# A graph network's last stage: scaled rows written into PSUM by VectorE, fewer tiles on GpSimd, shorter lags

## The reference, cut to what matters

```
out = node_feat + out                       # [10000, 512]
mean = out.mean(axis=0)
var = jnp.mean(jnp.square(out - mean), axis=0)
out = (out - mean) * jax.lax.rsqrt(var + EPS) * gamma + beta
...
x = _layernorm(x + out, axis=-1)            # the final result
```

## Time and profile before

| what | us |
|---|---|
| three timed runs | 1425.49, 1428.08, 1439.34 |
| their median | 1428.08 |
| span of the profiled execution, first to last instruction | 1427.3 |
| the last stage in it, about | 1267 to 1427 |

### The profile page before, as it was taken

How to read it: one execution, slowest core, us unless ns; L and a number is a source line. 1 busy time by engine, 2 the same in 40 slices (tenths; PEclk the granted TensorE clock), 3 DMA queues, 4 the chain that set the end, 5 groups by cost and what they waited for, 6 DMA issues and landing times. The chain is left out here.

```text
span 1427.3 us, 22061 instructions
## 1 busy us (share of the span) xinstructions
PE 1338.5 (94%) x6660; PEld 1074.8 (75%) x6660; DVE 1094.3 (77%) x2043; ACT 592.2 (41%) x1107; POOL 824.9 (58%) x766
## 2 busy tenths in 40 slices
PE   7889899999999769999999999999999999859897
PEld 6677778877778658888888888888888888634443
DVE  6468547888888713778888888888888888968787
ACT  3467544555555501222222223222222223246786
POOL 3456425666666533456556666666666665458785
PEclk9999999999999979999999999999999999879999
DMA  8689765666666341344444444444444443849855
GB/s 275 219 295 314 244 243 168 219 221 220 220 215 226 140 141 45 107 131 134 133 134 134 133 133 133 133 133 133 133 133 133 133 133 93 284 162 373 299 194 185
DMA packets 128302, 257.97 MB, mean 181 GB/s; under 512 B 21459, under 2 KB 21907, under 8 KB 128114
## 3 DMA queue, kind: packets, MB, share of 16 engines
q1 hardware_dynamic: 97490, 175.31, 36.9%
q0 software_dynamic: 29920, 80.38, 18.1%
q10 hardware_dynamic: 832, 1.57, 0.3%
HBM read 197.18 MB, written 73.60 MB: 190 GB/s over the span
## 5 line engine op out<-in xcount | busy, mean ns | idle before, releaser
L206 PE MATMUL ps<-w_lo,w_hi 128*128 128x512 f32 (+2 forms) x1140 | 416.6, 365 | 22.0 <-DVE w_lo L1470 18.0
L207 PE MATMUL ps<-w_hi,w_lo 128*128 128x512 f32 (+2 forms) x1140 | 410.7, 360 | 0.0
L208 PE MATMUL ps<-w_hi 128*128 128x512 f32 (+2 forms) x1140 | 410.4, 360 | 0.0
L206 PEld LDWEIGHTS ps<-w_lo,w_hi 128*128 128x128 f32 x1140 | 217.5, 191 | 54.9 <-DVE w_lo L1470 18.4
L208 PEld LDWEIGHTS ps<-w_hi 128*128 128x128 f32 x1140 | 217.0, 190 | 32.3
L207 PEld LDWEIGHTS ps<-w_hi,w_lo 128*128 128x128 f32 x1140 | 217.8, 191 | 29.8
L1216 POOL TENSOR_TENSOR acc_x<-acc_x,node_rows 128x512 f32<-128x512 f32 x72 | 117.0, 1625 | 76.1 <-DMA node_rows<-x_table 71.9
L910 POOL TENSOR_TENSOR node_y<-node_z,node_x 128x512 f32<-128x512 f32 x79 | 101.9, 1290 | 100.1 <-issue 79.3
L206 PE MATMUL ps<-w_lo,agg_hi 128*128 128x512 f32 x316 | 125.5, 397 | 0.0
L208 PE MATMUL ps<-w_hi,agg_hi 128*128 128x512 f32 x316 | 125.5, 397 | 0.0
L207 PE MATMUL ps<-w_hi,agg_lo 128*128 128x512 f32 x316 | 125.4, 397 | 0.0
(11 more groups left out here) (264 smaller groups left out, 2928.2 us busy)
## 6 DMA issues: line engine op xcount, KB each, us to landing
node_x<-in_x SPq DMA_DIRECT2D x79, 256.0 KB
x_table<-node_x SPq DMA_DIRECT2D x79, 256.0 KB, 2.1
node_rows<-x_table SPq DMA_DIRECT2D x79, 256.0 KB, 8.1
coef_all<-coef_table SPq DMA_DIRECT2D x38, 512.0 KB
edge_part<-part SPq DMA_DIRECT2D x40, 256.0 KB
out_dram<-rows_over_w_lo SPq DMA_DIRECT2D x40, 256.0 KB
node_x<-in_ea SPq DMA_DIRECT2D x38, 256.0 KB
msg_table<-dst_rows_and_msg SPq DMA_DIRECT2D x38, 256.0 KB
```

What stands on the lines that cost most here:

```text
L206: pe.matmul(to, left[0], right[1], start=first, stop=False)
L207: pe.matmul(to, left[1], right[0], start=False, stop=False)
L208: return pe.matmul(to, left[0], right[0], start=False, stop=last)
```

## The change

For 59 of 79 tiles VectorE now writes u * scale into the PSUM bank, and TensorE accumulates `shift` and x1 on top of it, without u. The other 20 tiles (j % 4 == 2) are scaled in SBUF by GpSimd with a copy of the scale row, which ScalarE makes; for them TensorE sums shift, x1 and u. GpSimd adds nothing any more. Seven matmuls write every bank once at the start of the stage, so that later ones accumulate. The statistics follow after 2 steps in place of 3, the reciprocals after 4 in place of 6, the roots after 8 in place of 10 and the outputs after 11 in place of 12. The two biases of a pair are one instruction.

```diff
-    PAIR, NORM = 10, 12
-    ADD = 4
+    PAIR, NORM = 8, 11
+    STATS, PAIRED = 2, 4
+    LATE = 4
...
         def by_pool(j):
-            return j % 8 in (1, 4, 6)
+            return j % 4 == 2
...
 # GpSimd
-                for k in range(NT + ADD):
+                for k in range(NT + LATE):
                     if k < NT:
                         pool.wait_ge(u_ok, k + 1)
-                        wait(pool, us_ok, k - R + 1)
                         nc.gpsimd.indirect_dma_start(out=u(k), ...)
-                    j = k - ADD
+                    j = k - LATE
                     if j >= 0 and by_pool(j):
-                        pool.wait_ge(us_ok, j + 1)
-                        nc.gpsimd.tensor_tensor(u(j), u(j), x1(j), ALU.add).then_inc(add_ok, 1)
+                        pool.wait_ge(wide_ok, SCALE_ROW)
+                        pool.wait_ge(u_in[j % R], u_before[j % R] + 16 * (j // R + 1))
+                        nc.gpsimd.tensor_tensor(u(j), u(j), scale_row[:], ALU.mult).then_inc(pool_ok, 1)
...
 # TensorE
+                def write_whole(to):
+                    pe.matmul(to[:], g.w(g.w_hi, WO, 0, 0, P), g.w(g.w_hi, WO, 0), start=True, stop=True).then_inc(open_ok, 1)
+
+                for whole in sum_banks[0:5]:
+                    write_whole(whole)
                 pe.wait_ge(sums_ok, 2)
...
+                pe.wait_ge(split_ok, 6)
+                for whole in sum_banks[5:7]:
+                    write_whole(whole)
                 pe.wait_ge(shift_ok, K)
 
                 for j in range(NT):
-                    wait(pe, norm_ok, j - 6)
-                    pe.matmul(bank(j), ones_r[:], shift, start=True, stop=False)
                     if by_pool(j):
-                        pe.wait_ge(add_ok, pool_adds(j))
+                        wait(pe, norm_ok, j - 6)
+                        pe.wait_ge(u_ok, j + 1)
+                        pe.matmul(bank(j), ones_r[:], shift, start=True, stop=False)
+                        pe.matmul(bank(j), g.ident[:], x1(j), start=False, stop=False)
+                        pe.wait_ge(pool_ok, scaled_by_pool(j))
+                        pe.matmul(bank(j), g.ident[:], u(j), start=False, stop=True).then_inc(sum_ok, 1)
                     else:
                         pe.wait_ge(u_ok, j + 1)
-                        pe.matmul(bank(j), g.ident[:], x1(j), start=False, stop=False)
-                        pe.wait_ge(us_ok, j + 1)
-                    pe.matmul(bank(j), g.ident[:], u(j), start=False, stop=True).then_inc(sum_ok, 1)
+                        pe.wait_ge(us_ok, scaled_in_psum(j))
+                        pe.matmul(bank(j), ones_r[:], shift, start=False, stop=False)
+                        pe.matmul(bank(j), g.ident[:], x1(j), start=False, stop=True).then_inc(sum_ok, 1)
...
 # ScalarE
+                act.wait_ge(wide_ok, SCALE_IN_PSUM)
+                nc.scalar.copy(scale_row[:], scale[:]).then_inc(wide_ok, 1)
                 for k in range(AHEAD, NT + NORM):
...
-                        act.wait_ge(scale_ok, 3 * (j // 2) + 2 + j % 2)
+                        act.wait_ge(scale_ok, 2 * (j // 2) + 2)
...
 # VectorE
-                dve.wait_ge(wide_ok, 1)
-                for k in range(NT + 7):
+                dve.wait_ge(wide_ok, SCALE_ROW)
+                dve.wait_ge(open_ok, 7)
+                for k in range(NT + PAIRED + 1):
                     j = k
-                    if j < NT:
+                    if j < NT and not by_pool(j):
                         dve.wait_ge(u_in[j % R], u_before[j % R] + 16 * (j // R + 1))
-                        v.tensor_tensor(u(j), u(j), scale[:], ALU.mult).then_inc(us_ok, 1)
-                    done = k - 6
+                        wait(dve, norm_ok, j - 6)
+                        v.tensor_tensor(bank(j), u(j), scale[:], ALU.mult).then_inc(us_ok, 1)
+                    done = k - PAIRED
...
-                    j = k - 3
+                    j = k - STATS
...
-                        for i in range(m, m + n):
-                            v.tensor_scalar(bias[:, i, :], mv[:, i, 0:1], rstd[:, i, :], -1.0, ALU.mult, ALU.mult).then_inc(scale_ok, 1)
+                        v.scalar_tensor_tensor(bias[:, m:m + n, :], mv[:, m:m + n, 0:1], -1.0, rstd[:, m:m + n, :], ALU.mult, ALU.mult).then_inc(scale_ok, 1)
```

More of the change, by code:

```diff
@@ L1798, in finish_stage @@
         ones_r = sb(ctx, "fin_ones", [P, P], F32R)
+        scale_row = sb(ctx, "fin_scale_row", [P, D])
         stats = sb(ctx, "fin_stats", [P, RM, 6])
@@ L1839, in finish_stage @@
         u_before = [landed(NT - 1 - s, 0, 0, 4) for s in range(4)] + [32 * ET // 4] * 2 + [32 * NB // 2] * 2
-        us_ok, add_ok, sum_ok, stat_ok, root_ok, scale_ok, norm_ok = (sem(n) for n in (
-            "fin_u_scaled", "fin_u_and_x_added", "fin_y_summed", "fin_stat", "fin_root_ok", "fin_scale_ok", "fin_norm"))
+        us_ok, pool_ok, sum_ok, stat_ok, root_ok, scale_ok, norm_ok = (sem(n) for n in (
+            "fin_u_scaled_in_psum", "fin_u_scaled_by_pool", "fin_y_summed", "fin_stat", "fin_root_ok", "fin_scale_ok", "fin_norm"))
+        open_ok = sem("fin_banks_written")
+        SCALE_IN_PSUM, SCALE_ROW = 1, 2
         y_out = g.w_in[2:6] + g.row_out + g.u_out
@@ L1899, in _ @@
                 pe.matmul(ps[2][:, 0:K], mirror[:], lo[:, 1, :], start=True, stop=True).then_inc(mirrored, 1)
+                pe.wait_ge(split_ok, 6)
+                for whole in sum_banks[5:7]:
+                    write_whole(whole)
                 pe.wait_ge(shift_ok, K)
                 for j in range(NT):
-                    wait(pe, norm_ok, j - 6)
-                    pe.matmul(bank(j), ones_r[:], shift[:].rearrange("p k n -> p (k n)"), start=True, stop=False)
                     if by_pool(j):
-                        pe.wait_ge(add_ok, pool_adds(j))
+                        wait(pe, norm_ok, j - 6)
+                        pe.wait_ge(u_ok, j + 1)
+                        pe.matmul(bank(j), ones_r[:], shift[:].rearrange("p k n -> p (k n)"), start=True, stop=False)
+                        pe.matmul(bank(j), g.ident[:], x1(j), start=False, stop=False)
+                        pe.wait_ge(pool_ok, scaled_by_pool(j))
+                        pe.matmul(bank(j), g.ident[:], u(j), start=False, stop=True).then_inc(sum_ok, 1)
                     else:
                         pe.wait_ge(u_ok, j + 1)
-                        pe.matmul(bank(j), g.ident[:], x1(j), start=False, stop=False)
-                        pe.wait_ge(us_ok, j + 1)
-                    pe.matmul(bank(j), g.ident[:], u(j), start=False, stop=True).then_inc(sum_ok, 1)
+                        pe.wait_ge(us_ok, scaled_in_psum(j))
+                        pe.matmul(bank(j), ones_r[:], shift[:].rearrange("p k n -> p (k n)"), start=False, stop=False, skip_group_check=True)
+                        pe.matmul(bank(j), g.ident[:], x1(j), start=False, stop=True, skip_group_check=True).then_inc(sum_ok, 1)
             @block.scalar
@@ L2007, in _ @@
                     if pair:
-                        dve.wait_ge(scale_ok, done // 2 + done // 2 * 2 + 1)
-                        for i in range(m, m + n):
-                            v.tensor_scalar(bias[:, i, :], mv[:, i, 0:1], rstd[:, i, :], -1.0, ALU.mult, ALU.mult).then_inc(scale_ok, 1)
+                        dve.wait_ge(scale_ok, done // 2 * 2 + 1)
+                        v.scalar_tensor_tensor(bias[:, m:m + n, :], mv[:, m:m + n, 0:1], -1.0, rstd[:, m:m + n, :], ALU.mult, ALU.mult).then_inc(scale_ok, 1)
                     if 0 <= j < NT:
```

6 lines of the change are left out of this document (4 added, 2 removed).

## The result

The change did not make the kernel faster. The ratio to the kernel before is 1.0038, with a 95% interval of 1.0020 to 1.0056 (medians 1438.03 and 1431.12 us, 20 runs each): by the ratio some 5 us slower, where 12 faster were forecast.

A forecast was written before the change was run, and what follows sets the result against it. GpSimd's queue was taken to set the pace, 1.746 us a tile. Gather 8 at 1283.1 plus 116.4 gives 1399.5; plus 8.6 and 6.9 makes 1415.0, with 0.8 for the runs' median 1416 us, range 1409 to 1425.

The forecast's parts named there:

- gathers 8 to 78: GpSimd's main term: 70 gathers at 1.31 and 17 operations at 1.16 make 111.4 us, plus 5 lost, 116.4.
- What could be late next: Check of other engines and new waits: TensorE 1.31 and VectorE 1.33 us a tile, both under GpSimd's 1.60.
- The paragraph on the Trainium skill: Two rules: SBUF contention leaves GpSimd's operation at 1.28 us; a TensorE left without work risks losing its full clock.
- Rival C: GpSimd's multiply costs 1.625 us, or the coupled lags cost as much: 6.8 us more, 1423; chance 0.12.
- signs of being wrong: GpSimd waiting for copies late, its waits before 1345 passing 8 us in sum, or TensorE's clock under 1.00 after 1290.
- its new pace: GpSimd in the steady part: (3 x 1.31 + 2.47)/4 = 1.60 us a tile, from 1.746.
- the price of the early bank writes: Stage start: five bank writes on TensorE ahead of the column totals delay VectorE's first step by 0.7 us (0 to 1).
- The start: Stage start to gather 8: at 1283.1 in place of 1284.28, a net gain of 1.2 us (bounds -1 and 2).
- VectorE's need: Steady part: two tiles fall from 3.05 to 2.66 us, 1.33 a tile, with the PSUM multiply taken as 0.66.
- The stalls before 1350: GpSimd's lost time in the first part, with DMA engines full: 5 us, one more than before.
- Rival A: The stalls vanish, since GpSimd no longer waits behind VectorE: 5 us less, 1411; chance 0.20.
- Rival B: Full DMA engines hold the first part at its old length, gather 43 staying at 1350.42: 1422 us; chance 0.19.

The follow-up runs named there:

- e1: The changed kernel with the merged bias undone, again two tensor_scalar instructions; ratio 0.9901 to the kernel before, pace 1.603 us a tile.
- e5: The changed kernel with all tiles scaled by VectorE, none by GpSimd, and two biases in place of the merged one; ratio 0.9881 to the kernel before.
- e6: The changed kernel with two biases again, plus an idle scalar_tensor_tensor with two small SBUF tensors that nobody reads; ratio 1.0048 to the kernel before.
- e14: The changed kernel with two biases, plus an idle scalar_tensor_tensor whose second tensor is read from PSUM; ratio 0.9862 to the kernel before.
- e10: The changed kernel with two biases, GpSimd scaling one tile of six, and the early bank writes behind the column totals; ratio 0.9887 to the kernel before.
- e4: The kernel before with only the shorter lags and its two biases; ratio 0.9987 to the kernel before.
- e12: The changed kernel with two biases and lags near the old ones (statistics 3, reciprocals 5, roots 10, outputs 12 steps); ratio 1.0010 to the kernel before.

## Why the prediction was wrong

The terms of the sum, each from the trace:

| term | forecast | changed | e1 |
|---|---|---|---|
| stage start to gather 8 | 15.8 | 17.2 | 17.2 |
| gathers 8 to 78 | 116.4 | 130.6 | 112.6 |
| gather 78 to the last statistics | 8.6 | 11.2 | 8.7 |
| to the end | 6.9 | 6.2 | 6.2 |
| stage | 147.7 | 165.2 | 144.7 |

**The step that failed** is "What could be late next", where the bias stands only as a gain: "one bias of about 0.1". Both halves of it were wrong. The gain is nothing, since the biases lie between statistics and aggregate (e5). And the merged instruction is the one new instruction with two SBUF tensors on VectorE beside a GpSimd that works on SBUF. Held, it took 1.74 us too long about every fourth tile. Between gathers 8 and 78 the changed kernel is 18.0 us longer than e1 and 14.2 longer than the forecast; in the tail it is 2.5 longer than e1. e1, e6 and e14 show this from three sides: without it the forecast's pace is there (1.603 against 1.60), the idle copy of it alone brings the loss back, and with one operand in PSUM it costs nothing.

The paragraph on the Trainium skill came closest and drew the wrong line. The Trainium skill's "GPSIMD Engine Reference", section Specifications, names contention with VectorE instructions that have two SBUF inputs. I applied it to the wide multiply and to GpSimd's price only, and both came out as said (GpSimd's 1.28 us, VectorE's 0.695). I did not go through the diff for the other instructions that it names, and did not ask which of the two engines waits. I also misread. The additions of GpSimd with a mean of 1.625 us did not run beside additions of VectorE with two SBUF tensors (L1532): in the trace none of those 72 overlaps a tensor_tensor of GpSimd. They ran beside a scan of VectorE's that reads two SBUF tensors, and that scan was slowed as well:

```profile
L1423 DVE TENSOR_TENSOR_SCAN v_turned<-coef_all,carry,v_turned x76: 725/1705/1802, 595.5 to 1240.3; 128x256 f32<-128x256 f32 x76
```

This is minimum, median and maximum in ns. Eleven of the 76 take 0.73 to 0.75 us; the other 65 take 1.66 to 1.80, and each of them overlaps a tensor_tensor of GpSimd (of the eleven, two do). That a VectorE instruction pays about 1 us for such a meeting stood in the trace of the kernel before. Rival C had 6.8 us for the wrong reason, so nothing of my list reached this case. One of the signs of being wrong did: GpSimd waited for copies in the late part, nine times and 10.9 us in all.

**Right:** that GpSimd's queue with its uncounted gaps set the pace before; its new pace; that TensorE and, in the steady part, the lags would not bind; the tail of e1 (8.7); and the price of the early bank writes, 0.7 forecast and 0.79 measured in e10. That e1's ratio of 0.9901 lies beside the forecast's 1416/1428.08 = 0.9915 is in part luck: its start took 1.4 us more than forecast, its gathers 8 to 78 3.8 less and its end 0.7 less.

**Mis-sized:**
- The start. 15.8 forecast, 17.2 measured in each kernel with the change in full. The trace of the changed kernel takes the 1.4 us apart. TensorE's first shift began 13.2 us after the stage's start, where the forecast's sum done at 1282.4 less 2.3 means 12.8; the sum of tile 0 took 2.5 and not 2.3; and gather 8 began 0.79 us after the end of its copy, where I had put next to nothing. The kernel before has the same 0.78 there.
- VectorE's need: 1.33 a tile forecast, 5.66/4 = 1.42 measured, as the multiply into PSUM takes 0.695 and not 0.66, and leaving out one bias saves nothing. Without effect at GpSimd's 1.60.
- The stalls before 1350: 5 us forecast. e1 takes 57.2 us for gathers 8 to 43, and 35 x 1.31 + 9 x 1.16 = 56.3 without any stall. Rival A was right in this: once GpSimd no longer waits behind VectorE, 0.9 us is left. The changed kernel's own 65.7 us looks like rival B, but the same loads pass in 57.2 in e1, so it was the hold. Rival B took a share near 1 for a full engine; the same stretch in e1 shows otherwise:

```profile
1300.00:1320.00 20.00, 18.32 (x45) 7.71 (x45) 17.39 (x56) 16.70 (x32) 16.39 (x17) 1.00 1.06 404
```

404 GB/s here, against 382 at a share of 1.05 and 331 at 0.91 in the earlier trace rows, and 371 at 1.00 in the changed kernel. So a share near 1 did not mean that no more could be moved.

- The end, from the last statistics. 6.9 forecast, 6.2 measured. e4, with the short lags alone, has 6.1, but e12, with the longer ones, has 5.9; why it got shorter stays open.
